# Four edits to a fused attention and expert kernel: first attention's masks and scores half by half, w2 loaded by fours, token rows in half floats, and separate buffers for the last tile

## The reference

```
x = x + attn0(norm(x), ctx, mask)              # 16 heads of 16; scores + mask * -10000, softmax, times ctx
x = x + ffn0(norm(x))                          # quantised gate/up/down
x = x + attn1(norm(x), ctx)                    # 16 heads of 64, wq/wk/wv/wo, then its own norm
x = x + experts(norm(x)):
    i = argmax(x @ Wr + br)                    # the token's expert
    relu(x @ W1[i] + b1[i]) @ W2[i] + b2[i]    # its own rows
    + sum over the other e of relu(b1[e]) @ W2[e] + b2[e]    # what an idle expert adds: a constant row
```

## Time and profile before

| what | value |
| --- | --- |
| three runs | 1381.17, 1379.34, 1378.74 us; median 1379.34 |
| the profiled execution | 1376.95 us, of which the span of the trace is 1375.2 |
| PE busy | 1302.9 us (95% of the span) |
| DVE / ACT / POOL busy | 1118.3 / 1034.2 / 398.7 us |
| stage a | masks of batch 0 at 10.41, of batch 31 at 223.47; stage b's first matmul at 245.63 |
| stage d | first instruction of its DVE chain at 1090.35, last scatter at 1372.66 |

### The profile page before, as it was taken

How to read it: one execution, slowest core, us unless ns; L and a number is a source line. 1 busy time by engine, 2 the same in 40 slices (tenths; PEclk the granted TensorE clock), 3 DMA queues, 4 the chain that set the end, 5 groups by cost and what they waited for, 6 DMA issues and landing times. The chain is left out here.

```text
span 1375.2 us, 34488 instructions
## 1 busy us (share of the span) xinstructions
PE 1302.9 (95%) x11262; PEld 1133.4 (82%) x11262; DVE 1118.3 (81%) x2014; ACT 1034.2 (75%) x2689; POOL 398.7 (29%) x674
## 2 busy tenths in 40 slices
PE   5999989999999999999899999999999589999998
PEld 2666656678887778899799999999998589999998
DVE  6889977879867889487677878778778868888887
ACT  3988878566579976663888888888887268888886
POOL 5555552000011111003222222222222134555543
PEclk9999999999999999999999999999999789999999
DMA  8411162385078999656023343243430375111210
GB/s 269 128 41 42 54 197 91 128 275 214 14 244 259 299 302 296 225 163 239 28 107 112 97 131 113 86 133 106 155 101 17 128 290 210 51 49 47 62 43 12
DMA packets 104021, 191.12 MB, mean 139 GB/s; under 512 B 12994, under 2 KB 68317, under 8 KB 99296
## 3 DMA queue, kind: packets, MB, share of 16 engines
q1 hardware_dynamic: 93248, 155.93, 33.7%
q0 software_dynamic: 10464, 33.57, 8.4%
q10 hardware_dynamic: 192, 0.13, 0.0%
HBM read 124.30 MB, written 68.03 MB: 140 GB/s over the span
## 5 line engine op out<-in xcount | busy, mean ns | idle before, releaser
L2362 ACT ACTIVATE c_w_raw<-c_ps_score,c_neg_max 128x128 f32<-128x128 f32 x512 | 181.9, 392 | 35.2 <-DVE c_neg_max L2161 27.5
L2706 PE MATMUL d_ps_hT<-d_zT,d_w_tile 128*128 128x128 f32 x1248 | 147.3, 277 | 2.5 <-DVE d_zT L2822 2.5
L2706 PEld LDWEIGHTS d_ps_hT<-d_zT,d_w_tile 128*128 128x128 f32 x1248 | 144.2, 193 | 3.2 <-DVE d_zT L2822 3.2
L2719 PE MATMUL d_ps_y<-d_w_parts,d_hT 128*128 128x256 f32 x936 | 121.7, 286 | 1.8 <-DVE d_res L2855 1.8
L2362 ACT ACTIVATION_READ_ACCUMULATOR c_w_raw<-c_ps_score,c_neg_max 128x1 f32 x512 | 118.5, 232 | 0.0
L2719 PEld LDWEIGHTS d_ps_y<-d_w_parts,d_hT 128*128 128x128 f32 x936 | 114.6, 191 | 2.0 <-DVE d_res L2855 2.0
L2889 ACT ACTIVATE d_h<-d_ps_hT,d_b1T 128x128 f32<-128x128 f32 x312 | 88.7, 367 | 32.3 <-PE d_ps_hT L2706 32.3
L2006 PE MATMUL c_ps_proj<-c_xnT,ahead_wq 128*128 128x256 f32 x768 | 107.2, 289 | 0.0
L2841 DVE TENSOR_TENSOR d_w_parts<-d_w,d_w_parts 128x1024 fp32r<-128x1024 f32 x78 | 95.3, 1222 | 11.0 <-ACT d_w_parts L2901 11.0
L2045 PE MATMUL c_ps_aux<-ahead_wo_high,c_attnT 128*128 128x256 f32 x512 | 99.6, 288 | 1.0 <-DVE logits L2185 1.0
L2006 PEld LDWEIGHTS c_ps_proj<-c_xnT,ahead_wq 128*128 128x128 f32 x768 | 95.2, 189 | 5.1 <-issue 5.0
(11 more groups left out here) (339 smaller groups left out, 3633.9 us busy)
## 6 DMA issues: line engine op xcount, KB each, us to landing
keys_scratch<-b_out SPq DMA_DIRECT2D x64, 256.0 KB, 4.6
values_scratch<-b_out SPq DMA_DIRECT2D x64, 256.0 KB, 3.8
ahead_kT<-keys_scratch SPq DMA_DIRECT2D x16, 1024.0 KB, 6.1
d_w<-w_in SPq DMA_DIRECT2D x16, 1024.0 KB, 7.1
split_scratch<-b_split SPq DMA_DIRECT2D x12, 1024.0 KB, 5.1
c_v_more<-values_scratch SPq DMA_DIRECT2D x24, 512.0 KB, 4.0
a_w<-w_in SPq DMA_DIRECT2D x64, 128.0 KB, 2.7
b_ctx_high<-split_scratch POOLq DMA_DIRECT2D x16, 512.0 KB, 5.4
```

Of the source, the lines that this page charges most:

```text
L2362: last = act.activation(prob[:, n, j, :], ps_score[:, n % 2, j, :], ACT.Exp, bias=neg_max[:, n, j:j + 1], accum_out=row_sum[:, n, j:j + 1])
L2706: last = pe.matmul(ps_hT[:, f, :], w1_tile[:, half, k, n * P:(n + 1) * P], zT[:, s, k, :], start=(k == 0), stop=(k == ND - 1))
L2719: last = pe.matmul(ps_y[:, 0:D], hT[:, s, a, f, :], w2_parts[:, half, b, n, :], start=(f == 0 and (a, b) == PARTS[0]), stop=(f == FB - 1 a ...
```

## The change

- Stage a, PE: `masks` and `scores` take a half. The order becomes mask of half 0, scores of q = 0 and 1, mask of half 1, scores of q = 2 and 3. `scores_done` is raised twice a batch; DVE's maximum of each half waits for its own.
- Stage a, SP: a piece of w2 (4 experts, 512 KB) is one transfer instead of four.
- Token rows: `at_row`, `numbers16` and `in_tile_hot` are in half floats (F16) instead of bf16. Batches 16 to 31 hold the number minus 4096 in one part; batches 0 to 15 keep two. 48 parts instead of 64. `place_rows` is cut and put elsewhere in DVE's list; the last `divide` of batch 31 moves ahead of `add_residual`.
- All eight constant rows are multiplied out at the end of stage c, four of them in the banks of `c_ps_probT`.
- Stage d: for tile 0, DVE copies z of the next tile before the low part of the hidden rows. The last tile has its own buffers for w2 (`w2_last`) and its own bank (`ps_last`); ACT rounds its first half of w2 ahead of the tile's relu.

```diff
-                        for j in range(4):
-                            sp.dma_start(w2[i][:, j, :], w2_dram[4 * g + j][:, f, :]).then_inc(w2_loaded, 16)
+                        sp.dma_start(w2[i][:, 0:4, :], w2_dram[4 * g:4 * (g + 1), :, f, :].rearrange("e p d -> p e d")).then_inc(w2_loaded, 16)
...
-                def masks(b):
-                    for half in range(2):
...
+                def masks(b, half):
...
-                def scores(b, u):
-                    pe.wait_ge(qT_ready, b + 1)
...
-                    for k, q in product(range(ND), range(NQ)):
+                def scores(b, u, half):
+                    if half == 0:
+                        pe.wait_ge(qT_ready, b + 1)
...
+                    for k, q in product(range(ND), range(2 * half, 2 * (half + 1))):
...
-                        masks(b)
-                        scores(b, u)
+                        for half in range(2):
+                            masks(b, half)
+                            scores(b, u, half)
...
-                    if half == 0:
-                        dve.wait_ge(scores_done, b + 1)
+                    dve.wait_ge(scores_done, 2 * b + half + 1)
...
+                        for first in range(NE // 2, NE, 2):
+                            sums_of_idle_rows(first)
...
+                        if t < NB // 2:
+                            dve.tensor_scalar(at_row[:, NB + t, :], prep["numbers16"][:], prep["slot_row"][:, t:t + 1], float(P * (t - NB)),
+                                              ALU.is_equal, ALU.mult)
+                        number = prep["token_no"][:] if t < NB // 2 else prep["token_back"][:, t:t + 1]
+                        dve.tensor_scalar(at_row[:, t, :], prep["numbers16"][:], prep["slot_row"][:, t:t + 1], number,
...
+                        place_rows(5, 6)
+                        divide(b, 3)
                     if back:
                         add_residual(b - 1, (u + 1) % 2, (w - 1) % RING)
...
+                    unhidden = isinstance(j, int) and j == 0
+                    if unhidden:
+                        copy_z(j + 1, (s + 1) % NS)
                     if inside(j, 0, NT - 1):
                         low_h(j, s, 0)
...
+        def w2_half(j, half):
+            return w2_last[half][:] if is_last(j) else w2_parts[:, half]
+
+        def y_bank(j):
+            return (ps_last if is_last(j) else ps_y)[:, 0:D]
...
+                    if is_last(j):
+                        round_w2(j, 0, e, loaded)
                     for half in range(2):
                         rectify(j, s, half, e)
-                    for half in range(2):
+                    for half in range(1 if is_last(j) else 0, 2):
                         round_w2(j, half, e, loaded)
```

More of the change, by code:

```diff
@@ L1761, in attention1 @@
         ps_rank = ps_proj[:, 0, 0:(NB + 1) * NE]
-        sums = [ps_proj[:, bank, e * D:(e + 1) * D] for bank in (1, 0) for e in range(2)]
+        sum_banks = [ps_proj[:, 1], ps_proj[:, 0]] + [ps_probT[:, n].rearrange("p h k -> p (h k)") for n in range(2)]
+        sums = [bank[:, e * D:(e + 1) * D] for bank in sum_banks for e in range(2)]
         xnT_rounded = sem("xnT_rounded")
@@ L2086, in sums_of_idle_rows @@
                         pe.wait_ge(ranks_taken, 1)
+                    if first >= NE // 2:
+                        pe.wait_ge(probT_ready, NU * NB)
                     for e in range(first, first + 2):
@@ L2312, in step @@
                         divide(b, 1)
+                    if isinstance(b, int) and b == NB:
+                        place_rows(6, 9)
                     if back:
@@ L2471, in experts @@
         sb("space_other", [P, NE, D])
[L2472 removed]
+        other = prep["other"]
         w1 = sb("w1", [P, NE, ND, FE])
@@ L2480, in experts @@
         assert nc.sbuf_base == EARLY_AT + EARLY_SIZE
+        hT_size = prod(hT.shape[2:]) * 4
+        w2_last = [nc.alloc_sbuf_tensor_at(f"d_w2_last{half}", [P, 2, FB // 2, D], F32R, offset=offset)
+                   for half, offset in enumerate((EARLY_AT + (NT - 3) % NS * hT_size, w1_tile_at))]
+        assert hT_size == 2 * FB // 2 * D * 4 == prod(w1_tile.shape[1:]) * 4
         sb("space_prep", [P, (prep_end - nc.sbuf_base) // 4])
@@ L2679, in _ @@
                         pe.wait_ge(at_row_ready, 1)
-                    for part in range(2):
-                        last = pe.matmul(ps_ids[:, 0:NT], at_row[:, part, t, :], in_tile_hot[:, t, :],
-                                         start=(t == 0 and part == 0), stop=(t == NB - 1 and part == 1))
+                    for row in ((t, NB + t) if t < NB // 2 else (t,)):
+                        last = pe.matmul(ps_ids[:, 0:NT], at_row[:, row, :], in_tile_hot[:, t, :], start=(row == 0), stop=(row == NB - 1))
                 last.then_inc(tokens_placed, 1)
-                for e in range(SUMS_EARLY, NE):
-                    last = pe.matmul(ps_other[:, e - SUMS_EARLY, :], all_but[:, e:e + 1].to_broadcast([2 * NE, P]), constant_rows[:],
-                                     start=True, stop=True)
-                last.then_inc(summed, 1)
                 def turn_z(j, s, i):
@@ L2711, in second_layer @@
                 def second_layer(j, s):
-                    if inside(j, 1, NT - 1):
+                    if inside(j, 1, NT - 1) and not is_last(j):
                         pe.wait_ge(res_ready, j)
@@ L2806, in _ @@
                 for t in range(LATE, NB):
-                    last = place_row(t)
+                    last = dve.tensor_scalar(at_row[:, t, :], numbers16[:], slot_row[:, t:t + 1], token_back[:, t:t + 1],
+                                             ALU.is_equal, ALU.mult)
                 last.then_inc(at_row_ready, 1)
```

130 lines of the change are left out of this document (65 added, 65 removed).

## The result

The changed kernel took 1407.58 us (median of four, 1403.78 to 1409.62), the kernel before beside it 1380.26 (1378.74 to 1381.41): 27.3 us more, ratio 1.0195, 95% interval 1.0169 to 1.0222. The profiled execution took 1409.62 with a span of 1407.9.

A forecast was written before the change was run, and what follows sets the result against it. It took stage a's closed loop of PE and ACT as the bound. Terms 33.6 - 5.35 - 1.3 - 1.2 - 1.0 - 1.6 = +23.1 on the median 1379.34 gave 1402.5 us, range 1391 to 1411.

The forecast's parts named there:

- The loop: Stage a: PE and ACT form a closed loop without DVE, so added mask and score time counts in full, 33.6 us.
- The price: Stage a: masks and scores by halves lengthen each batch by 1.16 us, bounds 0.88 and 1.35.
- rounds: Stage a scores: four rounds of 0.22 us per batch before; each half again needs four rounds, now of two instructions.
- The rival in which changes of mode are free: Stage a: new changes of tiling mode cost nothing, 25.5 us in place of 33.6, total 1394; chance 14%.
- w2 by fours, -5.35: Stage a, batch 28: fewer w2 issues on SP remove PE's wait for keys, saving 5.35 us; other end 0.
- The rival with the keys' wait kept: Stage a, batch 28: keys still wait behind w2's bytes in the transfer engines, total 1407.9; chance 10%.
- First batches, nothing: Stage a, batches 0 to 2: have waits of their own and add nothing, at most 3.5 us.
- End of stage c, -1.3: End of stage c: fewer token-row instructions ahead of the division PE waits for save 1.3 us, from 0 to 1.9.
- Head of stage d, -1.2: Start of stage d: six token-row instructions instead of twelve, and six fewer PE products, save 1.2 us together.
- tile 1, -1.0: Stage d, tile 1: z copied earlier shortens its wait of 2.01, saving 1.0 us, from 0 to 2.0.
- the other end: Head of stage d: gain of 0 if the gather behind it is held by the experts' weights.
- Last tile, -1.6: End of stage d: own w2 buffers and bank let PE start the last tile earlier, saving 1.6 us, 1.0 to 1.8.

The follow-up runs named there:

- e3_masks_first: The changed kernel with both halves' masks first, then the scores of half 0 and of half 1, each with its own count: 1370.24 us.
- e4_w2_only: The kernel before with only w2 in transfers of four rows of experts: 1373.66 us, ratio 0.9951.
- e2_halves_only: The kernel before with only the half-by-half masks and scores, w2 in single rows, stages c and d as before: 1410.55 us.
- e9_rows_behind: e3_masks_first with the token rows of blocks 6 to 8 placed behind the last output's logits instead of ahead of its last splitting: 1368.95 us.
- e10_both: e9_rows_behind with one expert's weights loaded ahead of stage d's gathers instead of two: 1369.03 us.
- e12_all: e10_both with each later half of an expert's weights waiting for the gather of one more tile: 1367.33 us.
- e6_one_early: e3_masks_first with one expert's weights loaded ahead of stage d's gathers instead of two: 1370.51 us.

## Why the prediction came out as it did

The forecast of 1402.5 lies 5.1 us under the measured 1407.58: its main step held, and some of the small ones did not.

- **The loop.** Right. The earlier trace rows named L657, masks, scores, L412 and L669 as the closed chain with DVE outside. ACT's idle time grew by the price of the scores (1.15), and nothing took any of it back.
- **The price.** Right in size (1.16; measured 1.15) and in its cause, the mask between halves that uses all rows: `e3_masks_first` takes away just that, and the price with it. The picture of "rounds" holds for a stretch between masks; what a stretch costs is the same for one, two or four groups of rows. The rival in which changes of mode are free needed a step of 7.5 and has fallen.
- **w2 by fours, -5.35.** The sum was right, but it was put down to the wrong one of two sufficient causes. The keys' wait goes by the transfers alone in fast steps (`e4_w2_only`) and by the slow steps alone without them (`e2_halves_only`). In this set the second was enough, so here the new transfers bought nothing; the prediction mentioned the longer steps only as a help. The rival with the keys' wait kept gave 1407.9, almost the measured time, but the wait was gone.
- **First batches, nothing.** Too low: 2.07 and 2.77, and in `e2_halves_only` 38.99 - 34.40 = 4.59, above the bound of 3.5. The bound took the price of a steady batch, but early on a half's scores last 2.08 in place of 1.13 (at 20.71 in the changed kernel). Part of these differences is not the change's: with both masks together the masks of batch 3 stand between 33.04 and 35.07 in ten profiles, the kernel before among them.
- **End of stage c, -1.3.** This step failed: 26.30 in place of 26.44, so -0.14. The prediction let the six rows use DVE's 1.47 of idle time. But with the wait ahead gone ACT's rounding came sooner too, the idle time was no longer there, and the rows stood on the path: `e9_rows_behind`, without them, starts the output 0.87 sooner. The clock, which the term left out, is in both profiles that give the -0.14: the kernel before had slow matmuls ahead of the output (1.12 for four L1983, 0.66 in the changed kernel), the changed kernel in it. Where the old order also had them in the output (`e2_halves_only`, `e4_w2_only`, each 4.45 us at 0.62), the stretch took 27.03 in both; the eight profiles with the new order took 26.14 to 26.62, a gain of 0.4 to 0.9. What sets the clock there stays open: the same wait of 0.96 was followed by 1.00 in `e9_rows_behind` and `e10_both` and by 0.62 in `e12_all`.
- **Head of stage d, -1.2, and tile 1, -1.0.** The chain did get 1.2 of it (1129.95 - 1121.15 = 8.80 to the gather's start, before 1100.32 - 1090.35 = 9.97), but the gather took 4.63 in place of 3.68, and from the chain's first instruction to the first transposes 0.2 was left (1134.63 - 1121.15 = 13.48, before 1104.04 - 1090.35 = 13.69); the prediction had given this as the other end. `e6_one_early` shows that the weights hold the gather. Tile 1's wait shrank by 1.5. What was gained was lost again further on, most of it at later gathers and the slow matmuls behind them: +3.55 in one profile, +0.45 in the other.
- **Last tile, -1.6.** Right (-1.68).

The two profiled executions differ by more (32.67) than the medians (27.3), since that of before lies 3.3 under its median and that of after 2.0 above. Of the 9.5 us between 32.67 and the sum, the head of stage d makes 5.75 (2.65 in the second profile), the first batches 2.1, the clock behind the last batch 1.4, and stages b and c 0.7; the loop came 0.4 under its term. Stages b and c, changed only at their end, varied by 2.3 between two profiles of one kernel; why is open. On the medians the forecast is 4.2 short of the difference. Which stretches hold these 4.2 can't be read, since only profiled executions show stretches.

## What to carry to other kernels

Before instructions that share the array by rows are split, look for what uses all rows between the parts: the number of such stretches sets the price, not how many groups work in one. A wait that is removed must be priced with all else that the change slows, since a slower loop can hide it by itself. And a gain ahead of a shared queue, or ahead of work that was filling an idle slot, is only half a gain: ask what stands behind it. When two profiles differ in a stretch, look at the granted clock there before the difference is put down to an edit.

## What was unexpected of the hardware

- A stretch of row-tiled matmuls between two uses of the full array took 1.12 to 1.17 us with 4, 8 and 16 instructions on one, two and four groups of rows.
- TensorE's granted clock was 0.79 over 40 us in which it was busy for 39.66, when its scores used one group of rows at a time; with two groups (38.30 busy) it was 1.00. Why is open.
- The same wait of 1.9 us behind the last batch of stage a was followed by a slow clock or not, 1.4 us apart: in the nine experiments with both masks together it was 23.6 us from the last masks to stage b in seven (granted clock 0.72 over the 6 us behind the wait) and 22.2 in two (`e4_w2_only`, `e12_all`; 1.00).
- The last output of stage c, the same instructions, took 2.95 to 2.97 us at a granted clock of 1.00 (the kernel before, `e9_rows_behind`, `e10_both`) and 4.26 to 4.46 at 0.62 to 0.65 in the eleven other profiles.
